# Decoder layer on one core: the feed-forward part in two unrolled blocks instead of ten, with the input quantised beside the gate's first round

## What is computed

```python
x = act_qdq(x)                                  # scale = max|x| / 32767 over the WHOLE tensor
up = act_qdq(x @ lpbq_dequant(w_up).T)          # 4096 x 512 @ 512 x 1536
gate = act_qdq(x @ lpbq_dequant(w_gate).T)
sig = fixed_qdq_u16(jax.nn.sigmoid(gate))
gate = act_qdq(gate * sig)
o = act_qdq(gate * up)
return o @ lpbq_dequant(w_down).T               # 4096 x 1536 @ 1536 x 512
```

## Time and profile before

| what | value |
| --- | --- |
| three timed runs | 3908.28, 3910.94, 3916.59 us (median 3910.94) |
| the profiled execution | 3914.25 us, of which the span of instructions is 3912.2 us |
| busy in the span | PE 84%, DVE 67%, ACT 57%, POOL 28% |
| mean granted clock of TensorE | 0.934 of full speed |
| feed-forward part | from 2,809 us to the end, some 1,103 us |
| of it, the products of gate, up and down | 2883.4 to 3155, 3168.5 to 3466, 3632.3 to 3904.1 |

### The profile page before, as it was taken

The page is one execution under the profiler, slowest core; times in us unless marked ns, Lnnn a source line. Parts: engine busy times, 40 slices in busy tenths (PEclk is TensorE's granted clock), DMA queues, the critical chain, the costliest instruction groups (busy, mean ns, idle before and its releaser), DMA issues. The chain is left out here.

```text
span 3912.2 us, 49399 instructions
## 1 busy us (share of the span) xinstructions
PE 3304.1 (84%) x15064; PEld 2528.0 (65%) x15064; DVE 2614.8 (67%) x4393; ACT 2226.1 (57%) x4058; POOL 1076.1 (28%) x1141
## 2 busy tenths in 40 slices
PE   5899999999999999478888888957559989930899
PEld 4687878787878787346555555635348867730687
DVE  5787777777777777356666667756543369966554
ACT  4676767676766676146666666751122234458665
POOL 1233333333333333225555555643200000000000
PEclk9999999999999999689999999988879999965999
DMA  4443443443434432364655555536532257789775
GB/s 124 125 148 117 133 132 123 128 133 118 146 116 132 127 119 87 114 98 97 114 103 101 107 106 112 82 109 216 183 106 102 105 183 269 268 311 372 251 249 187
DMA packets 281876, 582.31 MB, mean 149 GB/s; under 512 B 24488, under 2 KB 106416, under 8 KB 267328
## 3 DMA queue, kind: packets, MB, share of 16 engines
q1 hardware_dynamic: 268992, 554.57, 48.3%
q10 hardware_dynamic: 12672, 25.17, 1.7%
HBM read 339.49 MB, written 172.79 MB: 131 GB/s over the span
## 5 line engine op out<-in xcount | busy, mean ns | idle before, releaser
L640 POOL TENSOR_SCALAR sa_ex<-sa_ex,sa_rs 128x512 f32<-128x512 f32 x512 | 355.1, 693 | 952.2 <-DVE sa_rs L518 952.2
L1547 DVE TENSOR_REDUCE ca_negm<-ca_mx 128x1 fp32r<-128x512 f32 x512 | 352.7, 689 | 283.1 <-PE ca_mx L1688 275.1
L513 DVE TENSOR_REDUCE sa_nm<-sa_st 128x1 f32<-128x512 f32 x512 | 351.1, 686 | 268.5 <-PE sa_st L747 267.3
L389 ACT ACTIVATE sa_eh<-sa_tr 128x512 fp32r<-128x512 f32 x512 | 305.9, 597 | 293.2 <-PE sa_tr L757 289.9
L704 PE MATMUL sa_pj<-sa_xh,sa_w 128*128 128x512 f32 x1536 | 459.7, 419 | 11.4 <-DVE sa_kl L496 9.5
L1614 POOL TENSOR_TENSOR ca_el<-ca_ex,ca_eh 128x512 fp32r<-128x512 f32 x256 | 374.1, 1462 | 156.3 <-ACT ca_eh L1478 156.3
L382 ACT ACTIVATE sa_ex<-sa_st,sa_nm 128x512 f32<-128x512 f32 x512 | 350.8, 685 | 57.9 <-DVE sa_nm L513 54.5
L522 DVE TENSOR_TENSOR sa_el<-sa_tr,sa_eh 128x512 fp32r<-128x512 f32 x512 | 351.1, 686 | 35.9 <-ACT sa_eh L389 29.0
L1470 ACT ACTIVATE ca_ex<-ca_st 128x512 f32<-128x512 f32 x512 | 297.9, 588 | 65.2 <-PE ca_st L1706 63.4
L757 PE MATMUL sa_tr<-top_ident,sa_ex 128*128 128x128 f32 x2048 | 308.8, 273 | 0.2 <-POOL sa_ex L640 0.2
L757 PEld LDWEIGHTS sa_tr<-top_ident,sa_ex 128*128 128x128 f32 x2048 | 255.9, 141 | 72.4 <-POOL sa_ex L640 2.9
(11 more groups left out here) (242 smaller groups left out, 7521.6 us busy)
## 6 DMA issues: line engine op xcount, KB each, us to landing
sa_w<-w_split SPq DMA_DIRECT2D x56, 1536.0 KB, 7.4
up_g<-gate SPq DMA_DIRECT2D x50, 512.0 KB, 4.5
gate<-gate_ev SPq DMA_DIRECT2D x24, 1024.0 KB, 3.9
gate<-up_g SPq DMA_DIRECT2D x48, 512.0 KB, 2.8
up<-up_ev SPq DMA_DIRECT2D x24, 1024.0 KB, 5.6
mul_a<-gate SPq DMA_DIRECT2D x48, 512.0 KB, 11.8
mul_b<-up SPq DMA_DIRECT2D x48, 512.0 KB, 13.5
dn_a<-gate SPq DMA_DIRECT2D x96, 256.0 KB, 3.4
```

The lines of the kernel that those rows point to most:

```text
L389: nc.scalar.activation(eh[:, v % 2], tr[:, v % 2], ACT.Copy).then_inc(act_eh, 1)
L513: nc.vector.tensor_reduce(nm[:, u % U:u % U + 1], st[:, u % 2], AX_X, ALU.max, negate=True).then_inc(dve_mx, 1)
L640: nc.gpsimd.tensor_scalar(ex[:, u % U], ex[:, u % U], rs[:, u % U:u % U + 1], 1.0, ALU.mult, ALU.mult).then_inc(pool_n, 1)
L1547: nc.vector.tensor_reduce(negm[:, n % 2, qt, h:h + 1], mx[:, m % 2], AX_X, ALU.max, negate=True).then_inc(dve_mx, 1)
```

## The change

The ten blocks become two. `gate_up_stage` now holds the scale of x, the quantising, the 12 rounds of gate, the scale of gate and the 12 rounds of up as one list of 24 rounds. `multiply_down_stage` holds the scales of silu and up, the maximum pass, the scale of the product and the down projection. All loops are written out. A scale is a few steps in these lists (`ScaleSteps`), with semaphores of their own.

The input is loaded straight into `xh` and rounded there batch by batch. The low part of even batches is made by VectorE as before; that of odd batches by GpSimd, for which ScalarE writes the integers once more as float32 (`widened`, into the memory of `g_buf`, which is free until the up rounds). TensorE's products of round 0 wait for each batch's high and low part. The first piece of gate for the up rounds is loaded during gate's last round. In the second block the ring of the maximum pass has 4 places and not 6; the down projection has buffers of its own for its loads, so that SyncE issues its first four chunks right behind the last piece of the maximum pass. The transposed down weights use the second half of the PSUM that the down projection sums in.

```diff
+class ScaleSteps:
+    def __init__(self, nc, sp, sc):
+        self.nc, self.sc = nc, sc
+        self.row_done = sp.sem(f"{sc.name}_row_done")
+        self.all_done = sp.sem(f"{sc.name}_all_done")
+        self.set = sp.sem(f"{sc.name}_set")
+    def row(self):
+        self.nc.vector.tensor_reduce(self.sc.row[:, :], self.sc.partial[:, :], AX_X, ALU.max).then_inc(self.row_done, 1)
+    def across(self, e):
+        e.wait_ge(self.row_done, 1)
+        self.nc.gpsimd.partition_all_reduce(self.sc.all[:, :], self.sc.row[:, :], P, RMAX).then_inc(self.all_done, 1)
+    def finish(self, e):
+        e.wait_ge(self.all_done, 1)
+        self.nc.vector.tensor_scalar(self.sc.scale[:, :], self.sc.all[:, :], 1.0 / QMAX, 1e-12,
+                                     ALU.mult, ALU.max).then_inc(self.set, 1)
+        e.wait_ge(self.set, 1)
+        self.nc.vector.reciprocal(self.sc.inverse[:, :], self.sc.scale[:, :]).then_inc(self.set, 1)
+    def wait(self, e):
+        e.wait_ge(self.set, 2)
+def gate_up_stage(nc, env):
...
+            def load_gate(j, n):
+                if j:
+                    e.wait_ge(g_out[n], 16 * j)
+                else:
+                    e.wait_ge(pool_xl, B // 2)
+                e.wait_ge(out[n // 2], 16 * (j + 1))
+                e.dma_start(g_buf[:, n], gate_at(j, n)).then_inc(g_in[n], 16)
...
+            load_weights(0)
+            load_weights(1)
+            for b in range(B):
+                e.dma_start(f32(xh[tokens(b)]), env["xn3"][tokens(b)]).then_inc(x_in[b], 16)
+            for r in range(ROUNDS):
+                j = r - FT
+                if r + 2 < ROUNDS:
+                    load_weights(r + 2)
+                for n in range(PIECES):
+                    ahead, jn = (n + 2) % PIECES, j + (n + 2) // PIECES
+                    if 0 <= jn < FT:
+                        load_gate(jn, ahead)
+                    if j >= 0:
+                        store_silu(j, n)
+                    if n % 2:
+                        store(r, n // 2)
...
+            def product(r, b):
+                if B * r + b >= BANKS:
+                    e.wait_ge(act_ev, B * r + b - BANKS + 1)
+                for n, (ww, xx) in enumerate(((w_hi, xh), (w_lo, xh), (w_hi, xl))):
+                    if r == 0 and n == 0:
+                        e.wait_ge(act_xh, b + 1)
+                    if r == 0 and n == 2 and b % 2:
+                        e.wait_ge(pool_xl, b // 2 + 1)
+                    if r == 0 and n == 2 and b % 2 == 0:
+                        e.wait_ge(dve_xl, b // 2 + 1)
+                    for k in range(DK):
+                        last = nc.tensor.matmul(acc[:, b % BANKS], ww[:, r % 2, k], xx[:, k, b * S:(b + 1) * S],
+                                                start=(n == 0 and k == 0), stop=(n == 2 and k == DK - 1))
+                last.then_inc(pe_acc, 1)
...
+            def high_input(b):
+                e.wait_ge(dve_xq, b + 1)
+                nc.scalar.activation(xh[tokens(b)], qi[:, b % 2], ACT.Copy).then_inc(act_xh, 1)
+                if b % 2:
+                    if b >= 5:
+                        e.wait_ge(pool_xl, b // 2 - 1)
+                    nc.scalar.activation(widened(b), qi[:, b % 2], ACT.Copy).then_inc(act_xf, 1)
...
+            high_weights(0)
+            for b in range(AHEAD):
+                high_input(b)
+            x_scale.wait(e)
+            for r in range(ROUNDS):
+                if r == FT:
+                    g_scale.wait(e)
+                for b in range(B):
+                    if r == 0 and b + AHEAD < B:
+                        high_input(b + AHEAD)
+                    evict(r, b)
+                    if b == 5 and r + 1 < ROUNDS:
+                        high_weights(r + 1)
+                    if r >= FT and b % 2:
+                        sigmoid(r - FT, b // 2)
+        @block.gpsimd
+        def _(e):
+            x_scale.across(e)
+            for b in range(1, B, 2):
+                e.wait_ge(act_xf, b // 2 + 1)
+                nc.gpsimd.tensor_tensor(xl[tokens(b)], widened(b), f32(xh[tokens(b)]), ALU.subtract).then_inc(pool_xl, 1)
+            g_scale.across(e)
...
+            def quantise_input(b):
+                e.wait_ge(x_in[b], 16)
+                if b >= 2 and b % 2:
+                    e.wait_ge(act_xf, b // 2)
+                elif b >= 2:
+                    e.wait_ge(dve_xl, b // 2)
+                nc.vector.tensor_scalar(qi[:, b % 2], f32(xh[tokens(b)]), xsc.inverse[:, 0:1], None,
+                                        ALU.mult).then_inc(dve_xq, 1)
+            def low_input(b):
+                e.wait_ge(act_xh, b + 1)
+                nc.vector.tensor_tensor(xl[tokens(b)], qi[:, b % 2], f32(xh[tokens(b)]), ALU.subtract).then_inc(dve_xl, 1)
...
+            x_scale.row()
+            weights_tile(0)
+            low_weights(0)
+            x_scale.finish(e)
+            x_scale.wait(e)
+            quantise_input(0)
+            quantise_input(1)
+            low_input(0)
+            weights_tile(1)
+            for b in range(2, B):
+                quantise_input(b)
+                if b % 2 == 0:
+                    low_input(b)
+            for r in range(ROUNDS):
+                j = r - FT
+                if 0 < r and r + 1 < ROUNDS:
+                    weights_tile(r + 1)
+                if r == FT:
+                    e.wait_ge(dve_mx, 2 * FT)
+                    g_scale.row()
+                    g_scale.finish(e)
+                    g_scale.wait(e)
+                    nc.vector.tensor_scalar(c1[:, :], gsc.scale[:, :], 1.0 / 65536.0, None, ALU.mult).then_inc(c_done, 1)
+                    e.wait_ge(c_done, 1)
+                if j >= 0:
+                    quantise_gate(j, 0)
+                    quantise_gate(j, 1)
+                    silu(j, 0)
+                    quantise_gate(j, 2)
+                    silu(j, 1)
+                maxima(r, 0)
+                if r + 1 < ROUNDS:
+                    low_weights(r + 1)
+                if j >= 0:
+                    quantise_gate(j, 3)
+                    silu(j, 2)
+                    silu(j, 3)
+                maxima(r, 1)
+def multiply_down_stage(nc, env):
...
-    RING = 6
+    RING, QR, DR = 4, 4, 4
...
+            def load_chunk(i):
+                g, k = i // FT, i % FT
+                at = slice(g * S, (g + 1) * S)
+                if i >= DR:
+                    e.wait_ge(act_dq, 2 * (i - DR) + 2)
+                e.dma_start(da[:, i % DR], env["gate"][k, :, at]).then_inc(dab_in[i % DR], 16)
+                e.dma_start(db[:, i % DR], env["up"][k, :, at]).then_inc(dab_in[i % DR], 16)
...
+            load(0)
             load_weights(0)
+            for m in range(1, TOTAL):
+                if m >= RING and (m - RING) % EACH == 2 and (m - RING) // EACH + 1 < HT:
+                    load_weights((m - RING) // EACH + 1)
+            for i in range(CHUNKS):
+                load_chunk(i)
+                if i % FT == 0:
+                    load_residual(i // FT)
...
+            for i in range(CHUNKS + 1):
+                if i == 0:
+                    quantise_chunk(0)
+                    quantise_chunk(1)
+                if 2 <= i + 1 < CHUNKS:
+                    quantise_chunk(i + 1)
+                if i < CHUNKS:
+                    high(i)
...
+            s_scale.row()
+            u_scale.row()
+            s_scale.finish(e)
+            u_scale.finish(e)
...
+            e.wait_ge(c_done, 2)
+            o_scale.row()
+            o_scale.finish(e)
+            o_scale.wait(e)
+            nc.vector.tensor_tensor(c3[:, :], c2[:, :], osc.inverse[:, :], ALU.mult).then_inc(c_done, 1)
+            e.wait_ge(c_done, 3)
+            for i in range(CHUNKS + 1):
+                if i < CHUNKS:
+                    quantise(i)
+                if i:
+                    low(i - 1)
+                if i % FT == 3 and i > FT:
+                    output(i // FT - 1)
+            output(B - 1)
...
 def feed_forward(nc, env):
-    scale_stage(nc, env["x_scale"])
-    with ExitStack() as ctx:
-        for part in ("hi", "lo"):
-            env[f"xq_{part}"] = ctx.enter_context(nc.sbuf_tensor(f"xq_{part}", [P, DK, T], F32R))
-        quantise_input_stage(nc, env)
-        gate_up_stage(nc, env, "gate")
-        scale_stage(nc, env["gate_scale"])
-        gate_up_stage(nc, env, "up")
-    scale_stage(nc, env["silu_scale"])
-    scale_stage(nc, env["up_scale"])
-    with ExitStack() as ctx:
-        for part in ("hi", "lo"):
-            env[f"wd_{part}"] = ctx.enter_context(nc.sbuf_tensor(f"wd_{part}", [P, FT, D], F32R))
-        multiply_stage(nc, env)
-        scale_stage(nc, env["prod_scale"])
-        down_stage(nc, env)
+    gate_up_stage(nc, env)
+    multiply_down_stage(nc, env)
```

More of the change, by code:

```diff
@@ L1970, in _, with load_weights @@
-            for h in range(2):
-                e.wait_ge(out[h], 16 * FT + 16)
-                e.wait_ge(w_in[h], 16 * (FT // 2) + 16)
-            if side:
```

(56 more changed lines are left out.)

513 lines of the change are left out of this document (173 added, 340 removed).

## The result

Median 3841.6 us of 4 runs (3839.7 to 3846.8) against 3910.8 (3908.3 to 3916.6): ratio 0.982, 95% interval [0.9807, 0.9832], a gain of 69.2 us where 66 were forecast. The profiled run took 3839.68 us (span 3837.9, before 3912.2). The changes in the table are those of the two profiled runs, and add up to 74.3.

| from, to | before | after | change | forecast |
|---|---|---|---|---|
| start, scale of x | 2814.10 | 2818.60 | +4.5 | 0 |
| scale of x, gate's eighth product brought out | 93.7 | 64.4 | -29.3 | -29.4 |
| that, gate's last maximum | 245.5 | 246.1 | +0.6 | +1 |
| that, first step on a sigmoid | 26.7 | 10.1 | -16.6 | -16.5 |
| that, up's last maximum | 286.7 | 278.1 | -8.6 | -4.3 |

The account below looks back on a forecast made before the run. TensorE sets the pace in gate and down, VectorE in up; gains lie mostly at the seams. Terms -28.4, -17.8, -3.0, -3.5, -13.3 sum to -66.0, from 3910.94 to 3845 us; 8 in 10: 3828 to 3872.

Parts of the forecast that it names:

- Term 1: Start of gate: quantising beside the first gate round, eighth product out 29.4 us earlier, 1 us lost to the lower clock.
- without blocking: Rival at the input's quantising: GpSimd and VectorE don't block each other, 9 us more gained, 3836; chance 0.13.
- without overlap: Rival at the start of gate: quantising doesn't overlap the first round, gain there about 10 us, 3863; chance 0.05.
- Term 2: Seam of gate to up: first step on a sigmoid 16.5 us earlier, and a wait of 1.3 us gone.
- Term 3: Up rounds: written-out loops cut VectorE's idle time before silu's reductions, 3 us gained (bounds 0 and 6.3).
- Terms 4 and 5: Up to the maximum pass, first transfer 3.5 us earlier; maximum pass to down, first matmul 13.3 us earlier.
- The ring of 4: Rival in the maximum pass: four places starve the transfers, +58 us, 3903, or half-way 3874; chance 0.08.
- Term 6: Down's 96 chunks and the tail: the same instructions, so 0 us of change.
- Instruction supply: Rival in the written-out streams: pauses of TensorE's weight loads, +28 us at the mean, +193 at the longest; chance 0.06.

Follow-up runs that it names:

- e3: Kernel after the change with all low parts of the input on VectorE, without GpSimd's subtractions and ScalarE's float32 copies: 3821.9 us, ratio 0.9774.
- e4: Kernel before the change with only the loops of gate and up written out, all blocks kept: 3909.1 us, ratio 0.999.
- e5: Kernel before the change with gate and up loops written out and no weight tile behind the last round: 3906.4 us, ratio 0.9985.
- m2: Only strings of 48 products on zeros, layer left out, at chosen address sets: 11.20 us with the addresses of before, 10.92 with those of after.

## Why the prediction was right, and where not

**Term 1** (-29.4, and +1 for the clock): -29.3 and +0.6. The blocking is shown by VectorE's 4.66 beside GpSimd's 4.60 (priced at 4.6) and its 4.33 and 4.37 for 2.29, 8.4 us in all, where the sum without blocking was 8.9 shorter. e3 shows what the split costs as a whole. A pair took 11.7 for 12.5, with hand-offs near 0 where I had 0.1 each, and VectorE waited 3.0 us for the input's second batch, which I had as landed: two errors that cancelled. The rivals without blocking and without overlap are refuted; products began at 2830.71, 45.6 us before GpSimd took up its last subtraction.

**Term 2** (-16.5, -1.3): -16.6, and -1.8 in up's first round. GpSimd's reduction followed at once, so no change of its configuration was exposed.

**Term 3** (-3): -3.8 over ten rounds, at the same step of VectorE as said; e4 has the same round without the rest of the change.

**A tile that I missed.** The old loops dequantise a thirteenth tile, since the loop body is the same in every round (`nj = (j + 2) % FT`). VectorE is the bound in up's last round too, which fell from 24.4 to 21.4: 0.4 by the hand-offs and 2.6 by the tile; e5 has 2.7. I read the diff's `if r + 1 < ROUNDS` as an edge case and put no price on it.

**Terms 4 and 5** (-3.5, -13.3): -4.2, -12.5, and +0.7 in the pass between. The 0.8 that term 5 lacks are ScalarE's: the first rounded product was there at 3564.50, and its high part was begun at 3565.29, behind the rounding of the next chunk. The ring of 4 did not starve: the second half lands in 7.6 us in place of 13.5, so most of those 13.5 was queueing, as argued. Terms 2, 4 and 5 rest on the two timelines alone; no run has one of these seams without the others.

**Term 6** (0) is the step that failed: -8.9. "The same instructions" was true and not enough. They read other addresses, and m2 shows that these alone set the spacing at 0.2333 or 0.2267; 1,152 products times 6.7 ns are 7.7 us of it. The other 1.2 are six more products at the lower clock at the head of down in the profiled run of before (14 against 8). Term 6 had neither.

**Instruction supply.** Not one wait of TensorE's products "until issue" in the 948 us from 2,890 to the end.

The sum missed 10.3 us of gain (the tile's 2.6 and the addresses' 7.7). The two profiled runs differ by 74.6 us, 8.6 more than the 66 forecast, although 4.5 were lost ahead of the change, in stages that it doesn't touch. The medians differ by 69.2 only: the profiled run of before lies 3.4 above its median, that of after 2.0 below. So the median came within 3.4 us of the forecast by some luck; the terms 1 to 5 were right by their mechanisms.

Still open: why the modulus is 256, and why differences other than 0 come out at four levels. In self-attention the short strings explain the small effect. Cross-attention, whose products stand 0.2329 apart, proves nothing against the rule: its buffers start alike modulo 256 bytes, but the loaded operand of its products with the values is 66 numbers wide, 264 bytes, and so lies 8 bytes further, modulo 256, from head to head. Whether that is why, no run shows.

## What to carry to other kernels

Before you give half of a job to GpSimd, write down the chain that its half lies in, and look whether VectorE reads two SBUF inputs meanwhile: here one engine alone was 20 us faster than the two, 8.4 of it for the blocking and the rest for the slower engine and its extra copy. When a stage's buffers are allocated anew, its time can move with not one instruction changed; in a long stream of such products, put loaded and streamed operand at the same address modulo 256 bytes; where shorter products interrupt it every few, expect little. And when a loop is written out, count what its wrapped last round did for nothing.

## What was unexpected of the hardware

Products of 128x128 by 128x512 in fp32r, granted clock 1.00, nothing else running: 226.7 ns apart where the operands' addresses agree modulo 256 bytes (16 sets of 16 in m2), 228.9 to 234.4 where they don't (38 of 38). Within a set the intervals repeat in a fixed pattern, such as 235, 231, 235, 232 (difference 32) or seven values from 228 to 241 (difference 128). A set with 0 took 3 to 10 products to settle behind four short products or another difference.
